# Summing edge messages into a node window: 40 matmuls of 32 output rows each, or 24 matmuls of 128, 64 and 32 output rows

## What is computed

```python
gs = f_s[edge_src]                     # 64 scalars of the source node
gv = f_v[edge_src]                     # 32 vectors
y0 = edge_attr[:, 0]
y1 = edge_attr[:, 1:4]
mid0 = w0 * gs * y0[:, None]                                   # 64
mid1 = w3 * jnp.einsum('euc,ec->eu', gv, y1) * INV_SQRT3       # 32
mid2 = (w1 * gs)[:, :, None] * y1[:, None, :]                  # 64 x 3
mid3 = w2[:, :, None] * gv * y0[:, None, None]                 # 32 x 3
seg = lambda x: jax.ops.segment_sum(x, edge_dst, num_segments=N) * inv
ns0, ns1, nv2, nv3 = (seg(mid0), seg(mid1), seg(mid2), seg(mid3))
```

## Time and profile before

| | |
|---|---|
| median of 3 executions | 6857.24 us (6851.31 to 6891.02) |
| profiled execution | 6857.24 us, its span 6852.8 us |
| PE busy | 5973.2 us (87%), 76733 matmul records |
| PE weight loads busy | 4680.6 us (68%) |
| POOL busy | 4509.3 us (66%) |
| DVE busy | 4121.9 us (60%) |
| ACT busy | 2382.4 us (35%) |
| mean granted TensorE clock | 0.877 of full speed |

### The profile page before, as it was taken

One profiled execution on the slowest core, in us unless ns is written; L12 is line 12 of the kernel. 1 busy time (PEld: TensorE's weight loads), 2 busy tenths in 40 slices (PEclk: granted clock), 3 DMA queues, 4 the chain that ended last, 5 costly groups with the idle time before them and its releaser, 6 DMA issues. The chain is left out here.

```text
span 6852.8 us, 222659 instructions
## 1 busy us (share of the span) xinstructions
PE 5973.2 (87%) x76733; PEld 4680.6 (68%) x76733; DVE 4121.9 (60%) x11420; ACT 2382.4 (35%) x6454; POOL 4509.3 (66%) x4226
## 2 busy tenths in 40 slices
PE   6888889787888859999999999999965888999998
PEld 3666666566666648778787777777754763677776
DVE  5555555344444437777777777777756876444443
ACT  2122222112222226666666666666640012111111
POOL 1677777577777758888878888888830001677776
PEclk9999998788888869898889989899877965899999
DMA  1444444344444434444444444444424720455554
GB/s 60 117 129 126 128 126 129 101 130 128 129 127 127 127 78 81 82 83 83 82 79 82 84 82 82 82 84 82 82 65 127 204 64 21 129 141 140 139 139 120
DMA packets 810623, 719.97 MB, mean 105 GB/s; under 512 B 249162, under 2 KB 682298, under 8 KB 809826
## 3 DMA queue, kind: packets, MB, share of 16 engines
q0 software_dynamic: 263424, 321.38, 22.7%
q1 hardware_dynamic: 547042, 396.45, 20.5%
HBM read 557.61 MB, written 159.75 MB: 105 GB/s over the span
## 5 line engine op out<-in xcount | busy, mean ns | idle before, releaser
L892 POOL DMA_INDIRECT l_edge_g<-node_table,l_edge_idx x2352 | 2280.4, 970 | 1094.1 <-issue 752.6
L938 PE MATMUL l_edge_win_ps<-l_edge_hot,l_edge_prod 128*32 128x40 f32 (+1 forms) x47040 | 1256.5, 231 | 329.4 <-DVE sums_T L752 224.4
L938 PEld LDWEIGHTS l_edge_win_ps<-l_edge_hot,l_edge_prod 128*32 128x32 f32 x47040 | 1182.5, 118 | 506.3 <-issue 438.2
L1866 POOL DMA_INDIRECT att_g<-node_table,att_ends x784 | 1244.9, 1588 | 238.8 <-issue 238.5
L966 ACT ACTIVATE l_edge_h<-l_edge_h_ps 128x256 f32<-128x256 f32 (+1 forms) x784 | 342.2, 437 | 2478.9 <-PE l_edge_h_ps L913 2260.4
L1002 DVE TENSOR_TENSOR l_edge_prod<-l_edge_w_ps,l_edge_g 128x512 f32<-128x512 f32 x588 | 406.2, 691 | 1275.4 <-DMA l_edge_g<-node_table,l_edge_idx 1058.5
L1859 POOL DMA_INDIRECT att_g<-node_table,att_ends x784 | 792.1, 1010 | 275.8 <-issue 247.2
L1886 PE MATMUL att_turn<-ident,sums_T 128*128 128x128 f32 (+1 forms) x4704 | 764.3, 305 | 30.4 <-ACT sums_T L1971 23.9
L1971 ACT ACTIVATE sums_T<-att_turn 128x512 f32<-128x512 f32 (+1 forms) x1176 | 664.2, 591 | 203.1 <-PE att_turn L1886 197.5
L920 PEld LDWEIGHTS l_edge_w_ps<-l_edge_wo,l_edge_h 64*128 64x128 f32 (+1 forms) x4704 | 516.3, 196 | 295.6 <-issue 254.3
L1886 PEld LDWEIGHTS att_turn<-ident,sums_T 128*128 128x128 f32 (+1 forms) x4704 | 563.1, 152 | 204.0 <-issue 116.9
(11 more groups left out here) (269 smaller groups left out, 9538.1 us busy)
## 6 DMA issues: line engine op xcount, KB each, us to landing
l_edge_hot<-hot_tiles SPq DMA_DIRECT2D x392, 320.0 KB
hot_tiles<-l_edge_hot SPq DMA_DIRECT2D x196, 320.0 KB
l_messages<-att_rows SPq DMA_DIRECT2D x196, 320.0 KB
sum_msg<-l_messages SPq DMA_DIRECT2D x196, 320.0 KB, 3.6
l_edge_g<-node_table,l_edge_idx POOLq DMA_INDIRECT x2352
att_g<-node_table,att_ends POOLq DMA_INDIRECT x1568
att_ea<-in_edge_attr_T SPq DMA_DIRECT2D x196, 64.0 KB
l_scores<-att_score SPq DMA_DIRECT2D x784, 2.0 KB
```

What stands on the lines that cost most here:

```text
L892: pool.indirect_dma_start(g[s][:, t, :], None, rows_of, bass.IndirectOffsetOnAxis(idx[s][:, t:t + 1], 0)).then_inc(fetched[s], 16)
L938: return nc.tensor.matmul(win[n * VC:(n + 1) * VC, block * W:(block + kinds) * W], q[:, t, lo:lo + VC], to[:, t, kind:kind + kinds, :], st ...
L1866: pool.indirect_dma_start(g[s1][:, t, :], None, table[3], bass.IndirectOffsetOnAxis(ends[s1][:, TG + t:TG + t + 1], 0), compute_op=ALU.add ...
```

## The change

The window sums are written as 24 matmuls per group. Block 0 takes 128 stationary columns at once (`S0` and the following, width P) with 40 moving columns; the `S1` part takes 64 stationary columns with 120 moving ones; the third component of one product takes 32 with 40, and the twelve `V3` matmuls 32 with 40, now into output rows 64:96 in place of 96:128. Each of the four lists is done for all four tiles before the next. Since the `V3` sum lies in rows 64:96, the tails' matrix `w2` is filled in rows SC:MID (64:96) instead of MID:P, its matmul in `post_sums` contracts 96 rows instead of 128, its scaling reads a column of `row_scale`, and L3's preparation loads two tensors fewer. (`place` with its copies is unchanged.)

```diff
@@ edge_stream, tensor engine
-                                def add(n, block, t, lo, kind, kinds=1, opens=False):
-                                    return nc.tensor.matmul(win[n * VC:(n + 1) * VC, block * W:(block + kinds) * W],
-                                                            q[:, t, lo:lo + VC], to[:, t, kind:kind + kinds, :],
-                                                            start=opens, stop=True, skip_group_check=True)
-                                for t in range(TG):
-                                    for n in range(2):
-                                        add(n, 1, t, S1 + n * VC, 1, XYZ, opens=t == 0)
-                                for t in range(TG):
-                                    add(3, 2, t, V3, 1, opens=t == 0)
-                                    add(0, 0, t, S0, 0)
-                                    add(3, 2, t, V3 + VC, 2)
-                                    add(1, 0, t, S0 + VC, 0)
-                                    add(3, 2, t, V3 + 2 * VC, 3)
-                                    add(2, 0, t, V0, 0, opens=t == 0)
-                                    add(3, 0, t, V0 + VC, 0)
-                                    ins = add(2, 1, t, V0 + 2 * VC, 0)
+                                sums = [(win[:, 0:W], S0, P, slice(0, 1)), (win[0:SC, W:(1 + XYZ) * W], S1, SC, slice(1, 1 + XYZ)),
+                                        (win[SC:MID, W:2 * W], V0 + 2 * VC, VC, slice(0, 1))]
+                                for at, lo, width, kinds in sums:
+                                    for t in range(TG):
+                                        nc.tensor.matmul(at, q[:, t, lo:lo + width], to[:, t, kinds, :], start=t == 0, stop=t == TG - 1)
+                                for c in range(XYZ):
+                                    lo = V3 + c * VC
+                                    for t in range(TG):
+                                        ins = nc.tensor.matmul(win[SC:MID, 2 * W:3 * W], q[:, t, lo:lo + VC], to[:, t, 1 + c, :],
+                                                               start=c + t == 0, stop=c + t == XYZ + TG - 2)
@@ post_sums
-                nc.tensor.matmul(whole, self.sums[:, 2, :], self.w2[:, :], start=False, stop=False)
+                nc.tensor.matmul(whole, self.sums[0:MID, 2, :], self.w2[0:MID, :], start=False, stop=False)
@@ place_last
-                rows = self.w2[MID:P, 0:1 + SC]
-                nc.vector.tensor_scalar(rows, rows, 3.0 ** -0.5, None, ALU.mult).then_inc(self.w_ready, 1)
+                rows = self.w2[SC:MID, 0:1 + SC]
+                nc.vector.tensor_scalar(rows, rows, row_scale[SC:MID, 0:1], None, ALU.mult).then_inc(self.w_ready, 1)
@@ TailL3
-                for n in self.T:
+                for n in ("L3_gnn_Wv_l2_a", "L3_gnn_Wv_l2_c"):
...
-                pe.wait_ge(self.w_loaded, 16 * 10)
-                for l2, l3, at in self.OUTS:
+                pe.wait_ge(self.w_loaded, 16 * 8)
+                for l2, l3, at, rows in self.OUTS:
```

More of the change, by code:

```diff
@@ L1117, in load_last @@
                 sp.wait_ge(self.w_zeroed, 4)
-                for w, rows, at in ((self.w0, slice(0, SC), slice(0, SC)), (self.w2, slice(SC, MID), slice(MID, P))):
-                    sp.dma_start(w[at, 0:1], A[first][rows, :]).then_inc(self.w_loaded, 16)
-                    sp.dma_start(w[at, 1:1 + SC], A[scalars][rows, :]).then_inc(self.w_loaded, 16)
+                for w, rows in ((self.w0, slice(0, SC)), (self.w2, slice(SC, MID))):
+                    sp.dma_start(w[rows, 0:1], A[first][rows, :]).then_inc(self.w_loaded, 16)
+                    sp.dma_start(w[rows, 1:1 + SC], A[scalars][rows, :]).then_inc(self.w_loaded, 16)
                 sp.dma_start(self.top[0:MID, :], A[vectors]).then_inc(self.w_loaded, 16)
@@ L1396, in make @@
                 self.coef = sbuf(ctx, f"{tag}_tail_coef", [P, 2, NT])
-                self.w_in = sbuf(ctx, f"{tag}_tail_w_in", [P, 608])
+                self.w_in = sbuf(ctx, f"{tag}_tail_w_in", [P, 544])
                 self.multiplied = sem(ctx, f"{tag}_tail_multiplied")
                 self.stored = sem(ctx, f"{tag}_tail_stored")
[L1401 to L1404, removed]
+            T = {"L3_gnn_Ws_l2_a": 0, "L3_gnn_Ws_l2_c": 96, "L3_gnn_Wv_l2_a": 192, "L3_gnn_Wv_l2_c": 320}
+            L = {"L3_gnn_Ws_l3": (448, SC), "L3_gnn_Wv_l3": (512, VC)}
+            OUTS = [("L3_gnn_Ws_l2_a", "L3_gnn_Ws_l3", 0, MID), ("L3_gnn_Ws_l2_c", "L3_gnn_Ws_l3", SC, MID),
+                    ("L3_gnn_Wv_l2_a", "L3_gnn_Wv_l3", 2 * SC, P), ("L3_gnn_Wv_l2_c", "L3_gnn_Wv_l3", 2 * SC + VC, P)]
             def sp_load(self, sp):
@@ L1415, in pe_prep @@
             def pe_prep(self, pe):
-                pe.wait_ge(self.w_loaded, 16 * 10)
-                for l2, l3, at in self.OUTS:
+                pe.wait_ge(self.w_loaded, 16 * 8)
+                for l2, l3, at, rows in self.OUTS:
                     src, width = self.L[l3]
-                    ins = nc.tensor.matmul(self.post_ps[:, at:at + width], self.w_in[0:MID, self.T[l2]:self.T[l2] + P],
+                    ins = nc.tensor.matmul(self.post_ps[0:rows, at:at + width], self.w_in[0:MID, self.T[l2]:self.T[l2] + rows],
                                            self.w_in[0:MID, src:src + width])
@@ L1442, in dve_maps @@
                 nc.vector.tensor_copy(both[0:SC, :, 0:SC], scalars[0:SC]).then_inc(self.w_ready, 1)
-                nc.vector.tensor_scalar(third[MID:P, :, 0:SC], scalars[MID:P], 3.0 ** -0.5, None, ALU.mult).then_inc(self.w_ready, 1)
+                nc.vector.tensor_scalar(third[SC:MID, :, 0:SC], scalars[SC:MID], row_scale[SC:MID, 0:1], None, ALU.mult).then_inc(self.w_ready, 1)
             def pe(self, pe, i, s, r):
```

## The result

| | before | after |
|---|---|---|
| median | 6872.28 us (4 executions) | 7132.68 us (4 executions, 7118.78 to 7139.69) |
| ratio to before | | 1.0377, 95% interval 1.035 to 1.0404 |
| span of the profiled execution | 6852.8 us | 7132.6 us |

The account below looks back on a forecast made before the run. POOL was taken to bound all three edge passes, with PE becoming the bound in l3 and narrowly l0. 205 (l3) + 29 (l0) + 0 (l1) + 15 (clock), about +249 us on 6857.24, gave 7105 us, range 7020 to 7210.

Parts of the forecast that it names:

- POOL sets the pace before: All three edge passes: POOL's gathers take 22.7 us per four groups in l0, 23.3 in l1, 20.0 in l3.
- The window sum: PE, each group: 3.12 us to the next start against 1.84; +1.19 us in l0 and l3, +1.28 in l1.
- the 128-wide list: Block 0 in the window sum: 8 records at 0.112 us, paced by weight loads, 0.90 us.
- The 64-wide list: S1 part of the window sum: 8 records of 120 columns, loading hidden behind streaming, 0.80 to 0.82 us.
- the 32-wide records: Last lists of the window sum, rows 64:96: 32 records of 40 columns, load and stream overlapping, 1.12 us.
- In l1 the price: Pass l1: +1.28 us a group, PE at 20.9 us per four groups under POOL's 23.3, so 0 added.
- The quads: Time per four groups: PE's 24.2 us passes POOL's 20.0 in l3, +205; 23.3 passes 22.7 in l0, +29; l1 0.
- low clock in l0 and l1 together: Remaining low-clock stretches in passes l0 and l1 cost more once PE has no slack: +15 us.
- The clock: PE's granted clock rises with less idle time, above 0.95 in l0 and above 0.9 in l1.
- The rival in which the low clock stays: Passes l0 and l1: low clock keeps shares of about 18% and 32%, +180 us, about 7270; chance 0.10.
- Strips side by side: Window sum: 32-wide lists run beside the 64-wide one, about +1.0 us a group, 7025 to 7040 us; chance 0.09.
- Not slower: Window sum: record count sets its time, 21 ns each, so 48 take 1.1 us; total stays 6857; chance 0.05.

Follow-up runs that it names:

- interleaved: Kernel before with its 40 window-sum matmuls reordered, 120-column ones between 40-column ones of other strips: 6870.02 against 6869.84 us, ratio 0.9998.
- pool_more_before: Kernel before with one more small tensor_scalar on POOL per group, its result never read: ratio 1.019, median up 129 us.
- bias_on_dve: Kernel before with the tails' small bias product on DVE instead of POOL: 6749.55 us, ratio 0.9821.
- wide_moving: Kernel after with 120 instead of 40 moving columns in the 128-wide list: 7152.84 us, ratio 1.0414 to the kernel before.
- pool_more_after: Kernel after with one more small tensor_scalar on POOL per group, its result never read: 7163.11 us, ratio 1.0413 to the kernel before.
- s1_strips: Kernel after with the 64-wide list as two 32-wide ones side by side, 16 records for 8: ratio 1.0205 to the kernel before.
- block0_strips: Kernel after with block 0 as four 32-wide matmuls per tile instead of one 128-wide: 7005.31 us, ratio 1.0207 to the kernel before.

## Why the prediction was right, point by point

**POOL sets the pace before: shown.** A shorter window sum gives nothing (interleaved), 0.2 us more on POOL costs 0.2 us a group in each pass (pool_more_before), 0.86 less on it gives 0.8 for each tail product in l0 and l1 (bias_on_dve).

**The window sum: right to 0.02 us in l3 and l0, in part by errors that cancel.** Forecast were 3.12 us to the next start, and 0.095 less before it since the shape no longer changes on entering. Measured: 3.14, and from L920 to the window sum 6291.80 - 6290.40 = 1.40 us where it was about 1.49. The increment was 1.21 us a group ((24.25 - 19.41) / 4), forecast 1.19. L939 fits too, 6293.99 - 6291.80 = 2.19 us where the sum has 0.90 + 0.82 + 0.28 + 2 x 0.095 = 2.19, and L943 with 0.96 us has 0.84 + 0.095. But inside L939 the terms were off. By the starts of the single records (6299.34 to 6302.48), the 128-wide list takes 0.91 us with the change of shape behind it, where the sum has 0.995: its first two records start only 0.04 us apart, the later ones 0.10 to 0.112. The 64-wide list takes 0.96 with its change, where the sum has 0.915, because the first record behind a change of shape lasts 0.05 longer, and the 32-wide records 1.26 with the last change, where it has 1.215. So -0.08, +0.05 and +0.05: that the sum is right to 0.02 is luck, that it is right to 0.1 is not. That the 128-wide list's pace is not the streaming's is shown by wide_moving; that it is its 128 stationary columns, by the same 40 moving columns at 0.112 us a record there and 0.036 with 32.

**In l1 the price was too low,** 3.24 us instead of 3.12. The timeline of PE in pass l1 after:

```profile
1800.55 2.45 PE L939 MATMUL l_edge_win_ps<-l_edge_hot,l_edge_prod 128*128 128x40 f32 x24
...
1803.79 0.69 PE L913 MATMUL l_edge_h_ps<-l_edge_ea,l_edge_wi 16*128 16x256 f32 x2
```

Behind L920's 64-row shape the second record of the 128-wide list starts 0.13 us after the first, in l3 0.04. PE's quad at the full clock was 21.5 us, not 20.9. It lay under POOL's 23, as was said.

**The quads: right.** l3 +210 (205 forecast), l0 +43 (29), l1 +10 (0), with 15 for low clock in l0 and l1 together: 53 measured where 44 stood. l0's quad is 23.2 us in most of the pass, as forecast. The further 14 us of l0 are the margin: 22.7 for POOL was a mean that holds its stalls too. Five waits before gathers, some 20 us over the usual 0.30 together, stand in l0 before, and as many after. Without them POOL's quad is 22.3 us, and 49 x (23.2 - 22.3) = 44. pool_more_after agrees: it shows POOL's own quad to be 22.4 us or less in l0, since 0.8 us more a quad cost nothing there under PE's 23.2. What makes l1 10 us longer stays open: s1_strips, with a shorter window sum, took 1152.2 us there, and block0_strips 1138.8.

**The clock: right.** 0.98 and 0.93, forecast above 0.95 and 0.9. The rival in which the low clock stays is out.

**Strips side by side: the rival did not come true, but the reason I gave was wrong.** I wrote that the lists are issued in order and so only one record can lie beside another list. What keeps the lists apart in the kernel after is the change of shape: s1_strips, with one shape for both, lets eight records start beside and partly ahead of the list before them. The kernel before did so as well, with a record of the next list ahead of six. Its price for this case, 0.2 us a group, was too small; it is 0.5.

**Not slower:** out by block0_strips, where 32 records take 0.42 us.

**What fell** in the experiments is the size of two of POOL's terms (0.5 expected, 0.20 and 0.86 measured). In the prediction it is the terms inside the window sum, POOL's margin in l0 and the in-order rule for strips. Together they left the forecast change at +249 us where +260 was measured.

## What to carry to other kernels

Find the engine that sets the pace and its margin before weighing a change on another: here 1.2 us a group cost 210 us in the pass with a margin of 0.15, and 10 in the one with 1.9. For fp32 matmuls with few moving columns, count per strip of 32 output rows what it loads and streams, and the changes of shape between lists; here fewer, wider matmuls left strips idle and ran at the pace of their stationary columns, 0.112 us a record of 128. Between POOL's back-to-back gathers, the small instruction that waited for POOL's own result of a moment ago cost three times its length; look at the gap behind such an instruction, not at its length.

## What the runs showed of the hardware that I had not expected

- Matmuls of different 32-column strips start out of program order: in s1_strips a record of L942 started at 6207.64, with six records that precede it in the program starting at 6207.73 or later. In the kernel after, where the shape changes between the lists, every record of the group read started in program order.
- A change of shape costs 0.095 to 0.10 us between starts, from 128 to 64 (0.213 us where a record takes 0.112), from 64 to 32 (0.196 for 0.102) and on leaving (0.132 for 0.036) alike, all in the kernel after.
- On POOL an independent small instruction of 0.28 us lengthened the path by 0.2 us, and a dependent one of 0.27 us by 0.86: it waited 0.18 for its operand, and the gather behind it stood 0.58 us instead of 0.17.
- With 0.5 us less work a group the granted clock fell from 0.91, 0.84 and 0.99 to 0.84, 0.72 and 0.91, and with 1.2 us more it rose to 0.98, 0.93 and 1.00; the time followed neither where PE did not set the pace.
